# Unread identity products on TensorE ahead of its waits, in a cross-attention and soft-MoE kernel

## What is computed

```python
def reference(x, ctx, mask, wq, bq, wk, bk, wv, bv, wo, bo, norm_g, norm_b, slot_g, slot_b,
              scale, slot_embeds, Wg, bg, Wu, bu, Wd, bd):
    # cross-attention, 16 heads of 16
    q, k, v = split(ln(x) @ wq + bq), split(ctx @ wk + bk), split(ctx @ wv + bv)
    alpha = softmax(q @ k.T / 4 + (1 - mask) * -1e9)
    x = x + merge(alpha @ v) @ wo + bo
    # soft mixture of experts: 16 experts, 64 slots each, hidden width 512
    y = ln(ln(x)) * norm_g + norm_b
    se = (ln(slot_embeds) * slot_g + slot_b) * scale
    logits = einsum('bnd,esd->bnes', y, se)
    dispatch, combine = softmax(logits, over n), softmax(logits, over e and s)
    slots = einsum('bnd,bnes->besd', y, dispatch)
    hidden = gelu(slots @ Wg + bg) * (slots @ Wu + bu)        # per expert
    return x + einsum('bns,bso->bno', combine, hidden @ Wd + bd)
```

## Time and profile before

| what | us |
|---|---|
| median of 3 runs (lowest, highest) | 1158.82 (1156.41, 1159.63) |
| the profiled execution | 1161.87 |
| its span, first to last instruction | 1160.1 |
| mean granted TensorE clock, share of full | 0.969 |
| PE busy | 1064.4 (92%) |
| DVE, ACT, POOL busy | 700.1 (60%), 575.6 (50%), 332.3 (29%) |

### The profile page before, as it was taken

The page is one execution under the profiler, slowest core; times in us unless marked ns, Lnnn a source line. Parts: engine busy times, 40 slices in busy tenths (PEclk is TensorE's granted clock), DMA queues, the critical chain, the costliest instruction groups (busy, mean ns, idle before and its releaser), DMA issues.

```text
span 1160.1 us, 22281 instructions
## 1 busy us (share of the span) xinstructions
PE 1064.4 (92%) x7216; PEld 866.5 (75%) x7216; DVE 700.1 (60%) x1247; ACT 575.6 (50%) x1084; POOL 332.3 (29%) x348
## 2 busy tenths in 40 slices
PE   4788989999887887789999999999999999999997
PEld 3566767777653444478888888888888888888885
DVE  4556767777646888444555555655655555556544
ACT  1367768787665787733433343433424334333421
POOL 5258767676674434210010100100100100100000
PEclk8789999999998999789999999999999999999998
DMA  7858777787603544432142232432331331422122
GB/s 198 179 122 152 159 136 168 154 159 157 109 2 110 138 102 110 116 130 65 42 132 76 58 115 77 114 103 68 113 93 41 113 93 41 131 75 56 44 59 82
DMA packets 115080, 121.52 MB, mean 105 GB/s; under 512 B 46632, under 2 KB 105444, under 8 KB 115028
## 3 DMA queue, kind: packets, MB, share of 16 engines
q1 hardware_dynamic: 100908, 79.07, 30.8%
q0 software_dynamic: 10960, 40.67, 11.5%
q10 hardware_dynamic: 3160, 1.11, 0.6%
HBM read 73.87 MB, written 29.93 MB: 89 GB/s over the span
## 4 chain that ended last, share of the span: by engine, by line
PE 55%; DVE 1%; issue 1%; ACT 0%; DVEq 0%; ACTq 0%
PE down L1591 16%; PE gate L1551 15%; PE up L1551 15%; PE mix L1531 5%; PE mix L1524 4%; DVE gate_sb L1442 0%; ACT hid_h L1502 0%; DVE hid_l L1447 0%; DVE wd_l L1453 0%; DVE x L1427 0%; ACT gate_sb L1498 0%; DVE slot_l L1418 0%; DVEq L1645 0%; DVEq L1441 0%; DVEq L1424 0%
## 5 line engine op out<-in xcount | busy, mean ns | idle before, releaser
L1498 ACT ACTIVATE gate_sb<-gate,bgu 128x512 f32<-128x512 f32 x128 | 88.1, 689 | 222.3 <-PE gate L1551 207.7
L402 POOL TENSOR_TENSOR p_l<-p_f,p_h 121x800 f16<-121x800 f32 (+1 forms) x96 | 163.5, 1718 | 76.6 <-ACT p_h L652 75.9
L1502 ACT ACTIVATE hid_h<-gate_sb 128x512 fp32r<-128x512 f32 x128 | 80.9, 632 | 178.0 <-DVE gate_sb L1442 178.0
L1442 DVE SCALAR_TENSOR_TENSOR gate_sb<-up,bgu,gate_sb 128x512 f32<-128x512 f32 x128 | 95.9, 749 | 103.1 <-PE up L1551 101.3
L486 DVE TENSOR_REDUCE head_max<-at_rows 100x2 f32<-100x722 f32 x124 | 112.9, 910 | 70.5 <-PE at_rows L730 68.7
L1591 PE MATMUL down<-wd_h,hid_h 128*128 128x256 f32 x512 | 150.9, 295 | 0.7 <-DVE hid_l L1447 0.7
L1447 DVE TENSOR_TENSOR hid_l<-gate_sb,hid_h 128x512 fp32r<-128x512 f32 x128 | 88.6, 692 | 93.6 <-ACT hid_h L1502 93.6
L1591 PE MATMUL down<-wd_l,hid_h 128*128 128x256 f32 x512 | 145.0, 283 | 0.0
L1591 PE MATMUL down<-wd_h,hid_l 128*128 128x256 f32 x512 | 144.9, 283 | 0.0
L1275 POOL DMA_DIRECT2D wd<-in_Wd x16 | 12.3, 766 | 320.8 <-DVE eo L1465 300.4
L1591 PEld LDWEIGHTS down<-wd_h,hid_h 128*128 128x128 f32 x512 | 98.1, 192 | 3.4 <-issue 1.0
(11 more groups left out here) (167 smaller groups left out, 2269.1 us busy)
## 6 DMA issues: line engine op xcount, KB each, us to landing
eo_pair<-eo SPq DMA_DIRECT2D x128, 128.0 KB, 2.4
k_parts<-kq_n SPq DMA_DIRECT2D x16, 724.0 KB, 3.7
kt<-k_parts SPq DMA_DIRECT2D x32, 362.0 KB
wgu<-in_Wg POOLq DMA_DIRECT2D x16, 512.0 KB, 6.2
wgu<-in_Wu POOLq DMA_DIRECT2D x16, 512.0 KB, 6.9
wd<-in_Wd POOLq DMA_DIRECT2D x16, 512.0 KB, 5.2
combine<-combT SPq DMA_DIRECT2D x16, 400.0 KB, 4.2
dispatch<-dispT SPq DMA_DIRECT2D x16, 400.0 KB
```

The costliest lines, as they stand in the source:

```text
L402: nc.gpsimd.tensor_tensor(p_l[i][0:kn, :, 0:N], p_f[i][0:kn], p_h[i][0:kn, :, 0:N], ALU.subtract).then_inc(p_low, 1)
L1442: nc.vector.scalar_tensor_tensor(gate[c % 2][:], up_ps[c % 2][:], bu_col(bgu, pair, e, c), gate[c % 2][:], ALU.add, ALU.mult).then_inc(hid ...
L1498: nc.scalar.activation(gate[c % 2][:], gate_ps[c % 2][:], ACT.Gelu, bias=bg_col(bgu, pair, e, c)).then_inc(gelu_ready, 1)
L1502: nc.scalar.activation(hid_h[:, c, :], gate[c % 2][:], ACT.Copy).then_inc(hidh_ready, 1)
```

## The change

A function `stay_busy` issues `times` fp32 matmuls of the 128x128 identity by itself into a PSUM bank that is free at that point; nobody reads the result. They are issued ahead of TensorE's waits at these places (the nested function of the same name is renamed `value_products` and otherwise unchanged):

- attention, t=-3, -2, -1: 8, 2 and 4 ahead of xlT, 2 each ahead of q, 3 ahead of the product of bv and wo after step -3, 4 ahead of the keys at t=-1;
- attention, t=0: 6 ahead of the first cols product, with the wait for `seT_ready` moved ahead of them, and 2 ahead of the second;
- attention, t=B=16: 8 ahead of attT, 2 ahead of y;
- routing, through `keep_on`: 3 ahead of combT and 3 ahead of lT where t is 0 to 2 or 12 to 14 (combT from t=1, and at t=16), 3 ahead of xnT at t=-1 and 0, 5 ahead of the logits at t=12 to 14, 8 ahead of dispT at t=16;
- experts: 10 ahead of the first gate.

That is 45 in attention, 65 in routing and 10 ahead of the experts. No instruction is removed, and no other engine's program or DMA changes.

```diff
--- before.py
+++ after.py
@@ -57,6 +57,12 @@
 }
 OW = 3 * HD + 1
 V_GROUPS = [(0, 2), (2, 3)]
+
+
+def stay_busy(nc, keep, bank, times):
+
+    for _ in range(times):
+        nc.tensor.matmul(bank[:, 0:P], keep["ident"][:], keep["ident"][:], start=True, stop=True)
 
 
 def kc_size(j):
@@ -730,7 +736,7 @@
                     mm = nc.tensor.matmul(bank[0:N, c, 0:SW], q[0:ROWS_A, r, N * c:N * c + N], k[0:ROWS_A, r, :], start=True, stop=True)
                 mm.then_inc(s_done, 1)
 
-            def stay_busy(times):
+            def value_products(times):
 
                 pe.wait_ge(v_mid, 2 * B)
                 pe.wait_ge(v_res, 2 * B)
@@ -742,7 +748,11 @@
 
                 j, kn = u // 2, kc_size(u // 2)
                 if t >= B - 2:
-                    stay_busy(6 if u == 0 else 2)
+                    value_products(6 if u == 0 else 2)
+                if t == 0:
+                    if u == 0:
+                        pe.wait_ge(seT_ready, SC)
+                    stay_busy(nc, keep, out_ps[0], 6 if u == 0 else 2 if u < 2 else 0)
                 if u == 0:
                     pe.wait_ge(maxrow_in, 64 * (b + 1))
                 if u >= 1 or t >= 1:
@@ -766,7 +776,7 @@
                     if t >= 1:
                         pe.wait_ge(att_ready, b)
                 if t >= B - 2:
-                    stay_busy(1)
+                    value_products(1)
                 pe.wait_ge(p_low, NHALF * b + i + 1)
                 for e in range(HH):
                     h = (i % 2) * 4 + e // 2 + NPAIR * (e % 2)
@@ -782,6 +792,8 @@
                         pe.wait_ge(w_in["k"], 16)
                     turn = trip + (t + 3) // NBUF
                     pe.wait_ge(ctx_in[(t + 3) % NBUF], 16 * (turn + 1))
+                if t == -1 and c == 0:
+                    stay_busy(nc, keep, out_ps[0], 4)
                 if c == 1 and out:
                     pe.wait_ge(x1_ready, b)
                 if values and not (c == 1 and out):
@@ -819,6 +831,8 @@
                     if s == tab["k"][c]:
                         keys_proj(c)
                 if s == tab["xlT"]:
+                    if t < 0:
+                        stay_busy(nc, keep, out_ps[0], (8, 2, 4)[t + 3])
                     pe.wait_ge(xl_ready, p + 1)
                     pe.wait_ge(k_lo, 2 * p + 1)
                     for c in range(2):
@@ -827,6 +841,8 @@
                 if s == tab["q"]:
                     if t == -3:
                         pe.wait_ge(w_in["q"], 16)
+                    if t < 0:
+                        stay_busy(nc, keep, out_ps[0], 2)
                     pe.wait_ge(xlT_ready, p + 1)
                     for c in range(2):
                         for kc in range(2):
@@ -834,6 +850,8 @@
                     mm.then_inc(q_done, 1)
             if out:
                 if s == AT["attT"]:
+                    if t == B:
+                        stay_busy(nc, keep, proj[0], 8)
                     pe.wait_ge(att_ready, b)
                     if values:
                         pe.wait_ge(v_hi, 2 * n + 2)
@@ -844,6 +862,8 @@
                         mm = nc.tensor.transpose(attT_ps[:, c, :], att[:, c * P:(c + 1) * P], ident[0:N, 0:N])
                     mm.then_inc(attT_done, 1)
                 if s == AT["y"]:
+                    if t == B:
+                        stay_busy(nc, keep, proj[0], 2)
                     pe.wait_ge(attT_ready, b)
                     for kc in range(2):
                         mm = nc.tensor.matmul(y_ps, attT[:, kc, :], w["o"][:, kc, :], start=(kc == 0), stop=(kc == 1))
@@ -864,6 +884,7 @@
                 part(s + SLOTS, b - 1, t - 1, trip)
                 part(s, b, t, trip)
             if t == -3:
+                stay_busy(nc, keep, out_ps[0], 3)
                 pe.wait_ge(w_in["o"], 16)
                 pe.wait_ge(bvb_ready, 1)
                 for kc in range(2):
@@ -1137,11 +1158,21 @@
 
     @block.tensor
     def _(pe):
+        def keep_on(t, times):
+
+            if t <= 2 or B - 4 <= t < B - 1:
+                stay_busy(nc, keep, mix_first[0], times)
+            elif t >= B:
+                pe.wait_ge(lcopy_ready, B)
+                stay_busy(nc, keep, logits[:, 1, :], times)
+
         def part(s, b, t):
             weights, exps, logit, norm = stages(t)
             n = b + 1
             for g in range(2):
                 if weights and s == AT_RT["combT"][g]:
+                    if g == 0:
+                        keep_on(t, 3)
                     pe.wait_ge(ecomb_ready, b)
                     if t >= 2:
                         pe.wait_ge(dispT_ready, 2 * (b - 2) + g + 1)
@@ -1158,12 +1191,16 @@
                         mm = nc.tensor.transpose(lT_ps[:, g, j * N:(j + 1) * N], l_sb[:, s0:s0 + P], ident[0:N, 0:N])
                     mm.then_inc(lT_done, 1)
                 if weights and s == AT_RT["dispT"][g]:
+                    if g == 0 and t >= B:
+                        keep_on(t, 8)
                     pe.wait_ge(dispn_ready, b)
                     pe.wait_ge(combT_ready, 2 * (b - 1) + g + 1)
                     for j in range(SG):
                         mm = nc.tensor.transpose(out_ps[0:N, g, j * P:(j + 1) * P], disp_n[:, g * SG + j, :], ident[:])
                     mm.then_inc(dispT_done, 1)
             if logit and s == AT_RT["xnT"]:
+                if t <= 0:
+                    keep_on(t, 3)
                 pe.wait_ge(xn_ready, n + 1)
                 if t >= 0:
                     pe.wait_ge(xnT_ready, n)
@@ -1171,6 +1208,8 @@
                     mm = nc.tensor.transpose(xnT_ps[:, c, :], xn[:, c * P:(c + 1) * P], ident[0:N, 0:N])
                 mm.then_inc(xnT_done, 1)
             if logit and s == AT_RT["logits"]:
+                if t >= B - 4:
+                    keep_on(t, 5)
                 pe.wait_ge(xnT_ready, n + 1)
                 if t >= 0:
                     pe.wait_ge(lcopy_ready, n)
@@ -1538,6 +1577,8 @@
                 prev = not (first and h == 0)
                 for e in range(2):
                     u = 2 * hs + e
+                    if first and h == 0 and e == 0:
+                        stay_busy(nc, keep, up_ps[1], 10)
                     pe.wait_ge(sl_ready, 4 * hs + 4)
                     pe.wait_ge(wl_ready[e], pair + 1)
                     for c in range(FC):
```

## The result

The changed kernel takes 1161.71 us (median of 7 runs, 1158.85 to 1164.67) where the kernel before took 1157.5 beside it (7 runs): a ratio of 1.0033, 95% interval 1.0017 to 1.0049. Run again later, 12 runs against 35, it was 1160.28 against 1159.09, ratio 1.0007 (0.9990 to 1.0023). The median of the kernel before lies between 1157.5 and 1161.66 in the six comparisons of this document, so that times are read only against those taken beside them. I had forecast 1153.6, faster, with 1161 as the upper end.

What follows compares the result with a forecast made beforehand. TensorE bounds the experts, so earlier gains move the end equally. 2.0 + 1.8 - 0.7 + 0.8 + 2.3 - 1.0 = 5.2 us faster, from the median 1158.82 to 1153.6 us; 8-in-10 range 1147 to 1161.

Steps and rivals of the forecast that it cites:

- What bounds the kernel: Experts: TensorE is the limit and the change adds nothing after the first gate, so earlier gains move the end equally.
- I take +2.0: Attention's first steps, 35 products: 2.0 us faster, between -1.5 and +6.
- The danger: Second keys: their wait grows from 2.12 to some 3.3 us, the clock may fall, keys take near twice 2.67: -2.2.
- my bounds: Attention's first steps: the gain lies between -1.5 and +6 us.
- The 6 us that I gave the clock at most: Attention's first steps: first q 0.86, second to third q 2 at most, clock in later intervals 3.3 at most.
- Attention's end and routing's first steps: Attention's end (10 products) +1.8 us, with y and first logits at full clock; routing's first steps (21) -0.7.
- t=12 to 14: Routing's last steps, 33 products: +0.8 us; t=13 logits gain 2.3, t=14 loses 1.5; between -1.5 and +2.
- Routing's end: Routing t=16, 11 products: last dispT and two slot rounds at full clock, +2.3 us, between -0.4 and +2.5.
- half of that work at full clock and half of the products too: Ahead of the experts, ten products: 1.6 + 0.7 - 3.3 = -1.0 us; best +0.9, worst -3.5.
- the 1.6 + 0.7 of my sum: Ahead of the experts: the gains set against 3.3 us of products, giving -1.0.
- My slower rival: Barrier: clock falls, ten products at 0.43 cost 4.3 us, 1 comes back, -3.3; 5.7 slower in all, 1164.5; chance 0.10.
- The start doesn't pay: Transfers hold attention's first steps (+0), ends pay, experts cost 2: 2.2 us faster, 1156.6; chance 0.32.

Runs made afterwards that it cites:

- routing's last: Only the products of routing's steps t=12 to 14 (33) and t=16 (11), against the kernel before: 1157.61 us, ratio 0.9977 (0.9963 to 0.9990).
- the two ends: Only the products at attention's end, routing's steps up to t=2 and t=16, against the kernel before: 1157.83 us, ratio 0.9970; again 1158.38, 0.9967.
- the early products alone: Only the products of attention's steps t=-3 to -1, against the kernel before: 1162.2 against 1161.66 us, ratio 1.0000 (0.9982 to 1.0018).
- four of its places without the rest: Only products at attention's t=0, attention's end, routing's first steps and t=16, against the kernel before: 1155.69 against 1161.66 us, ratio 0.9941 (5 runs).

## Why the prediction was wrong, step by step

The means of each stretch over all profiles, and what my sum had (us, + is faster):

| stretch | without | with | worth | predicted |
|---|---|---|---|---|
| start of the span to the fourteenth y (attention's first steps) | 328.5 (10) | 329.0 (6); t=0 alone 325.5 (2) | -0.5; t=0 alone +3.0 | +2.0 |
| fourteenth to last y (the early products again) | 23.0 (13) | 24.1 (7) | -1.1 | 0 |
| last y to sixth logits | 43.0 (11) | 42.1 (9) | +0.9 | +1.1 (1.8 - 0.7) |
| 13th to 16th logits (t=12 to 14) | 27.0 (14) | 26.6 (6) | +0.4 | +0.8 |
| last logits to TensorE's first matmul behind the barrier | 23.8 (11) | 21.5 (9) | +2.3 | +2.3 |
| from there to the first down | 15.5 (15) | 18.0 (4); twenty 20.5 (1) | -2.4; twenty -4.9 | -1.0 |

(Profiles in brackets; those with x loaded late are left out of the first line.) The first line is the weakest: single profiles scatter over 325.9 to 330.6 us both with and without early products, and the two with t=0's alone have 324.0 and 327.0.

The lines add up to most of the ratios. By the table and as measured: attention's end with routing's first steps 0.9992 and 0.9987; routing's last 0.9977 and 0.9977; the experts' ten 1.0021 and 1.0017, twenty 1.0042 and 1.0042; all first steps 1.0014 and 1.0014; the two ends 0.9972 and 0.9970, again 0.9967, with t=0's products 0.9947 and 0.9941, with all first steps 0.9986 and 0.9993; without the first steps 0.9990 and 0.9995; t=12 to 14 alone 0.9997 and 0.9996; twice the first steps' products 1.0014, if the second dose costs nothing, and 1.0023; the early products alone 1.0014 and 1.0000. Besides the first comparison of the whole change, two intervals miss their sum: t=0's alone, 0.9974 and 0.9993 (0.9981 to 1.0004), and the change without first steps and experts, 0.9969 and 0.9989 (0.9974 to 1.0004).

**What bounds the kernel**: right; the stretch of the experts from the first to the last down is 631.6 us in all 20 profiles, so what came earlier moved the end by as much. (The stretch at the first expert is not the last at half clock, as I wrote: two short ones follow from 1150 us on, behind the last down.)

**Attention's first steps, "I take +2.0"**: the step that failed. By the table they are worth -1.6, with an uncertainty of some 2 us; that they gain 2.0 is ruled out by the run of them alone (1.0014, 0.9996 to 1.0032). Wherever kernels differ only by them, the one with them is slower: 1.0007 and 0.9995, 0.9993 and 0.9970.

The danger was named (the wait for v_r grows, the clock falls in it, the keys take near twice as long) and priced at -2.2, and came in every profile. The +2.0 beside it was a choice between my bounds and had no row of its own, and two things failed in it. The 6 us that I gave the clock at most were never to be had: VectorE sets when the second keys can start, and their end comes 1.2 us later with early products than without (31.1 and 29.9 us on the mean). And the price did not end there. The transfers that this stretch waits for stand behind these keys in SP's order, and the first cols, 58.8 us in the mean of the twelve profiles without early products, comes at 60.7 in the six with them, 1.9 later. TensorE's last work before that wait, products left out, ends no later (53.9 us with them, 54.5 without).

That the first cols is bound by transfers is shown from three sides. Doubled products left 2.49 us of the wait for the transfer where the single dose left 5.97, and the second batch's cols start where they did; the full clock from 33 us on that they brought did not start the first cols sooner; and the load of x moved back brought it forward, by 5.8 us against the one profile before and 4.9 against the mean. Behind the first cols most of the 1.9 us come back: by the fourteenth y 0.5 is left, less than the scatter.

The second part of the loss is the second line of the table, and it rests on two profiles: of the 7 with early products two took 26.0 and 26.5 us from the fourteenth to the last y, with the clock at half for 10 us there, the other five 22.9 to 23.5; of the 13 without them none took more than 23.4. Stretches of 3.4 us at half clock stand there in kernels without early products too. Two of seven don't show that early products make the clock fall 300 us later.

The products of t=0 are another matter, and I had put them into one sum with the others. They stand in front of the wait for the transfer itself. After it the clock came back sooner in the two profiles with them and no early ones: the half-clock stretch around the first cols ended at 56.8 and 62.8 us, in the ten without any at 61.8 to 69.6, 66.9 on the mean. They are worth 3.0 by these two profiles and by the ratios with and without them (0.9941 and 0.9967, whose intervals just touch), 0.8 by the run of them alone. So a gain is likely and its size open. The two halves don't add up to the whole either: -1.6 less 0.8 to 3.0 would leave the early products -2.4 to -4.6, and alone they measured 1.0000 (0.9982 to 1.0018), a loss of 2.1 us at most.

**Attention's end and routing's first steps**: right, both in y and logits and in the sum (+0.9 for +1.1). The count was short: of the 21 products of routing's first steps my terms price 18; three (0.7 us) are in none.

**t=12 to 14**: the logits of t=13 are at 3.68 as forecast, in all 6 profiles with these products, where the 14 without them have 5.2 to 6.2; so the clock is held and the products cost most of what it gives. The size is +0.4, less than the profiles scatter (26.2 to 28.2 without these products), and alone they measured 0.9996, not told from nothing. The version with the ends and without them did better (0.9970, 0.9967) than the one with them (0.9989), with intervals that overlap.

**Routing's end**: right to 0.1.

**The experts, "half of that work at full clock and half of the products too"**: mis-sized. No product ran at full clock: all ten took 4.6 us. What came back is the rest, 2.2 us; -2.4 instead of -1.0. The 2.2 is near the 1.6 + 0.7 of my sum, though its 0.7 had no row; the miss is the 3.3 that I took as the products' cost, which was 4.6. My slower rival had the place and the mechanism, with -3.3. By the Trainium skill ("TensorE: Matmul & The Clock Gate", "Part 1: The HAM clock gate") idling sends the gate to half rate and activity releases it. The trace agrees: TensorE idles some 4 us at the barrier and its clock falls, and with twenty products ahead of the gates it is back at full before the first gate, on products alone.

**The sum**: -1.6 + 0.9 + 0.4 + 2.3 - 2.4 = -0.4, a ratio of 1.0003. The second comparison's 1.0007 agrees, the interval of the first (1.0017 to 1.0049) leaves it out; what 1.5 us or more of that are stays open. The long stretch at 337.8 us is one such piece, in the profiled execution. Of the 5.6 us between my 5.2 and this sum, attention's first steps are 3.6 and the experts 1.4. Nor is it shown why the store of the second keys takes 4.6 to 5.3 us to land in six of the seven profiles with early products and 3.5 to 3.7 in the others; in the seventh, with twice the products, it takes 3.5.

My rival "The start doesn't pay" was the nearest, transfers and all; its 2.2 faster is 2.6 above the table's sum, of which the start is 1.6.

## What to carry to other kernels

Here a product that nobody reads paid only in front of a wait that it didn't lengthen and behind which useful work would have run at the lower clock. In front of ready work it was paid in full: ten took 4.6 us and gave back 2.2, twenty took 7.5 and gave back 2.6. Before placing such products, ask of each stretch what its end waits for: where that was a transfer, getting there sooner was worth nothing, and making TensorE quick ahead of a wait for another engine moved the fall of the clock into that wait. Judge them place by place: the whole change was worth nothing or less, and four of its places without the rest 6.9 us in five runs (6.2 by the table).

## What the runs showed of the hardware

The half-clock stretch at the barrier was 6.8 us long with 20 products in it, in all four profiles with 10, and in 13 of the 15 with none; in one of these it was 3.4 us, in one it had begun before the barrier. A product takes 0.23 us at the full clock (sixteen 3.73 us) and 0.46 at half (six 2.76). And executions of one code differ: in the ten profiles without any product in attention's first steps, the second batch's cols start between 78.1 and 82.7 us, so that one profile of each kernel can't tell a change of 2 us there. The first cols, at 59.85 us in the one profile that I had when I predicted, starts between 57.5 and 61.0 in the twelve without early products.
